# Moving the normalise and residual work of an attention and feed-forward kernel from VectorE to GpSimd, and its last projection one output later

## What is computed

```python
# B = 8, S = 256, D = 128, 16 heads of 8 numbers, hidden size 512
def layernorm(x, eps=1e-5):
    return (x - mean(x)) / sqrt(var(x) + eps)

def attn(x):
    q, k, v = split(x @ W_qkv + b_qkv)
    scores = q @ k.T / sqrt(8) + rel_bias[clip(i - j + 128, 0, 256)]
    return softmax(scores) @ v @ W_out + b_out

def ffn(x):                                  # ternary weights, a scale per output
    h = silu(x @ w1.T * w1_s) * (x @ w2.T * w2_s)
    h = gelu(h @ h1.T * h1_s)
    h = gelu(h @ h2.T * h2_s)
    return h @ w3.T * w3_s

x = x + layernorm(attn(layernorm(x)))
x = x + layernorm(ffn(layernorm(x)))
```

## Time and profile before

| | us |
|---|---|
| median of 3 executions | 291.42 (290.83 to 292.56) |
| the profiled execution | 292.18 |
| its span | 290.4 |
| PE busy | 268.5 (92% of the span) |
| DVE busy | 219.3 (76%) |
| ACT busy | 205.9 (71%) |
| POOL busy | 102.4 (35%) |

### The profile page before, as it was taken

How to read it: one execution, slowest core, us unless ns; L and a number is a source line. 1 busy time by engine, 2 the same in 40 slices (tenths; PEclk the granted TensorE clock), 3 DMA queues, 4 the chain that set the end, 5 groups by cost and what they waited for, 6 DMA issues and landing times.

```text
span 290.4 us, 5171 instructions
## 1 busy us (share of the span) xinstructions
PE 268.5 (92%) x1875; PEld 180.4 (62%) x1875; DVE 219.3 (76%) x442; ACT 205.9 (71%) x316; POOL 102.4 (35%) x107
## 2 busy tenths in 40 slices
PE   7999989899999999999998998899999999999980
PEld 7756645555555554565554554567887888888860
DVE  3489977889789889889889899848556843673674
ACT  2777777776786786885886876777469976896750
POOL 7616000103504305906966957018630202400111
PEclk9999999999999999999999999999999999999996
DMA  6979506232221263470320200000000000010012
GB/s 166 320 238 142 184 11 208 89 83 77 74 76 38 77 207 124 138 224 8 104 81 19 61 1 3 1 3 1 0 2 0 0 0 2 0 36 2 2 36 77
DMA packets 21356, 21.17 MB, mean 73 GB/s; under 512 B 3664, under 2 KB 18768, under 8 KB 21072
## 3 DMA queue, kind: packets, MB, share of 16 engines
q1 hardware_dynamic: 20464, 20.53, 24.8%
q10 hardware_dynamic: 864, 0.27, 0.4%
HBM read 14.90 MB, written 5.64 MB: 71 GB/s over the span
## 4 chain that ended last, share of the span: by engine, by line
PE 60%; DVE 22%; ACT 9%; issue 5%; DMA 1%; POOL 0%; SPq 0%; ACTq 0%; DVEq 0%
PE place L1441 10%; PE place L1442 10%; PE place L1244 8%; DVE mx L685 7%; PE pv L1296 6%; PE place L1236 4%; ACT ring L1008 4%; DVE y_and_z L620 4%; PE place L1270 4%; DVE stats L609 2%; PE place L1195 2%; DVE place L692 2%; ACT place L1015 2%; PE pv L1442 2%; PE pv L1441 2%
## 5 line engine op out<-in xcount | busy, mean ns | idle before, releaser
L685 DVE TENSOR_REDUCE mx<-place 128x4 f32<-128x1024 f32 x64 | 78.1, 1222 | 13.1 <-PE place L1244 11.8
L517 POOL TENSOR_TENSOR rstd<-mv,mhalf 128x2 f32<-128x2 f32 (+1 forms) x26 | 21.0, 809 | 153.0 <-DVE mv L617 153.0
L1008 ACT ACTIVATE ring<-place 128x1024 f32<-128x1024 f32 x64 | 65.6, 1027 | 6.3 <-PE place L1281 3.0
L1244 PE MATMUL place<-room,identr 128*128 128x512 f32 x128 | 46.9, 447 | 0.0
L1015 ACT COPY place<-raw 128x1024 f32<-128x1024 f32 x37 | 37.7, 1022 | 12.2 <-DVE mx L685 11.9
L1441 PE MATMUL place<-room,w_hi 128*128 128x512 f32 (+1 forms) x116 | 44.6, 387 | 0.7 <-DVE room L818 0.7
L1442 PE MATMUL place<-room,w_hi 128*128 128x512 f32 (+1 forms) x116 | 44.0, 382 | 0.0
L818 DVE TENSOR_TENSOR room<-ring,room 128x512 fp32r<-128x512 f32 x32 | 21.4, 690 | 18.5 <-ACT room L1096 18.5
L1296 PE MATMUL pv<-ring,vx 128*9 128x256 f32 x512 | 33.6, 380 | 0.0
L1270 PE MATMUL place<-room 33*128 33x256 f32 x256 | 31.7, 328 | 1.1 <-DVE place L692 1.0
L1236 PE MATMUL place<-room 33*128 33x256 f32 x256 | 28.3, 297 | 2.9 <-ACT ring L1008 2.7
(11 more groups left out here) (141 smaller groups left out, 442.9 us busy)
## 6 DMA issues: line engine op xcount, KB each, us to landing
raw<-ext SPq DMA_DIRECT2D x8, 384.0 KB, 6.9
room<-q_parts SPq DMA_DIRECT2D x48, 64.0 KB
room<-k_parts SPq DMA_DIRECT2D x48, 64.0 KB
w_lo<-h SPq DMA_DIRECT2D x2, 1024.0 KB, 5.2
q_parts<-w_hi SPq DMA_DIRECT2D x4, 256.0 KB, 3.0
k_parts<-w_hi SPq DMA_DIRECT2D x2, 512.0 KB, 3.4
xs<-x SPq DMA_DIRECT2D x3, 256.0 KB, 5.7
w_lo<-w SPq DMA_DIRECT2D x3, 256.0 KB, 2.7
```

Source lines behind the costliest of these rows:

```text
L517: nc.gpsimd.tensor_tensor(rstd[:, at:at + width], mv[:, at:at + width, 1], mhalf[:, 0:width], ALU.pow).then_inc(rstd_set, 1)
L685: nc.vector.tensor_reduce(mx[:, s // RPAIRS, :, :, s % RPAIRS].rearrange("p i k -> p k i"), max_tile(b * PAIRS + s)[:, :, :].rearrange("p ...
L1008: nc.scalar.activation(probs[:, s % PRING, :, :, :].rearrange("p k j n -> p (k j n)"), score_tile(b * PAIRS + s)[:, :, :].rearrange("p k n ...
L1244: last = mm(max_tile(b * PAIRS + s)[:, half, :], identr[:, :], windows(table_hi[:, 2 * s + half, :], 0, P, 2, S), start=False, stop=True, ...
```

## The change

1. POOL takes over the normalising of units 2, 3 and 4 of x, of y and of z, and the addition of the residual. DVE keeps the moments, now as `x1_moments(b - 1)` in slot 6 behind `maxima(b + 1, 6)`; POOL does for each sequence inv_std, two normalise instructions, the addition, inv_std, two normalise instructions, and then the pieces of the weights.
2. DVE normalises unit 0 of x before it takes the moments of unit 1; unit 1 is normalised behind `minus_ident`. POOL does two table copies between the inv_std of unit 1 and of unit 2.
3. PE does the last sequence's projection behind three outputs of layer 1 of chunk 1 in place of two.
4. A wait: before the moments of y of sequence b DVE waits for z of sequence b - 1, since both use the same mean and variance.

The core of the diff (`x_normalize`, `residual` and `second_norm` on DVE are deleted, but for `x_normalize` of units 0 and 1):

```diff
+            def normalize(dst, src, t, at=0):
+                return nc.gpsimd.tensor_scalar(dst, src, mv[:, at + t, 0:1], rstd[:, at + t:at + t + 1],
+                                               ALU.subtract, ALU.mult)
+            def x_normalize(u):
+                first, tiles = UNITS[u]
+                pool.wait_ge(rstd_set, u + 1)
+                if u >= 3:
+                    pool.wait_ge(xnT_ready, 2 if u == 3 else 4)
+                for t in range(tiles):
+                    last = normalize(x_norm[u][:, t, :], xs[:, first + t, :], t, first)
+                last.then_inc(xn_set, 1)
+            def residual(b):
+                inv_std(b * 2 + NU + 1, TPB)
+                pool.wait_ge(rstd_set, b * 2 + NU + 1)
+                for t in range(TPB):
+                    last = normalize(y[:, t, :], y[:, t, :], t)
+                last.then_inc(y_norm, 1)
+                pool.wait_ge(y_norm, b + 1)
+                xb = xs[:, TPB * b:TPB * b + TPB, :]
+                nc.gpsimd.tensor_tensor(xb, xb, y[:, :, :], ALU.add).then_inc(x1_set, 1)
+            def second_norm(b):
+                inv_std(b * 2 + NU + 2, TPB)
+                pool.wait_ge(rstd_set, b * 2 + NU + 2)
+                if b > 0:
+                    pool.wait_ge(zT_ready, b)
+                for t in range(TPB):
+                    last = normalize(z[:, t, :], xs[:, b * TPB + t, :], t)
+                last.then_inc(z_set, 1)
...
             x_inv_std(1)
+            table_high(0)
+            table_high(1)
             x_inv_std(2)
-            for s in range(PAIRS):
+            table_high(2)
+            x_normalize(2)
+            for s in range(3, 6):
                 table_high(s)
-                if s == 5:
-                    x_inv_std(3)
+            x_inv_std(3)
+            x_normalize(3)
+            table_high(6)
+            table_high(7)
...
             x_inv_std(4)
+            x_normalize(4)
...
                 if b > 0:
-                    inv_std((b - 1) * 2 + NU + 1, TPB)
-                    inv_std((b - 1) * 2 + NU + 2, TPB)
+                    residual(b - 1)
+                    second_norm(b - 1)
                 for piece in SPLIT_AT[b]:
                     split_weights(piece)
...
-            inv_std((B - 1) * 2 + NU + 1, TPB)
-            inv_std((B - 1) * 2 + NU + 2, TPB)
+            residual(B - 1)
+            second_norm(B - 1)
             gate_parts(3)
...
-            x_moments(1)
             x_normalize(0)
             dve.wait_ge(row_zeros, 1)
             dve.wait_ge(bq_scaled, 1)
             spread_weights(nc.vector.tensor_copy, 0, (0,))
+            x_moments(1)
...
-            x_normalize(1)
             dve.wait_ge(ident_loaded, 16)
             nc.vector.tensor_scalar(minus_ident[:, :], ident[:, :], -1.0, None, ALU.mult).then_inc(minus_set, 1)
+            x_normalize(1)
...
                 dve.wait_ge(y_read, b + 1)
+                if b > 0:
+
+                    dve.wait_ge(z_set, b)
                 moments(lambda t: y[:, t, :], TPB, b * 6 + base + 2)
...
+            def x1_moments(b):
+
                 dve.wait_ge(x1_set, b + 1)
                 moments(lambda t: xs[:, b * TPB + t, :], TPB, b * 6 + base + 4)
...
-                        if s == 5:
-                            residual(b - 1)
                         if s == 6:
-                            second_norm(b - 1)
+                            x1_moments(b - 1)
...
-                whole(layer1, 1, exact, (0, 1))
+                whole(layer1, 1, exact, (0, 1, 2))
                 project(B - 1)
-                whole(layer1, 1, exact, (2, 3))
+                whole(layer1, 1, exact, (3,))
```

More of the change, by code:

```diff
@@ L630, in x_normalize @@
                 dve.wait_ge(rstd_set, u + 1)
-                if u >= 3:
-                    dve.wait_ge(xnT_ready, 2 if u == 3 else 4)
                 for t in range(tiles):
@@ L716, in attn_moments @@
                 dve.wait_ge(y_read, b + 1)
+                if b > 0:
+                    dve.wait_ge(z_set, b)
                 moments(lambda t: y[:, t, :], TPB, b * 6 + base + 2)
-            def residual(b):
-                dve.wait_ge(rstd_set, b * 2 + NU + 1)
-                for t in range(TPB):
-                    last = normalize(y[:, t, :], y[:, t, :], t)
-                last.then_inc(y_norm, 1)
-                dve.wait_ge(y_norm, b + 1)
-                xb = xs[:, TPB * b:TPB * b + TPB, :]
-                nc.vector.tensor_tensor(xb, xb, y[:, :, :], ALU.add).then_inc(x1_set, 1)
+            def x1_moments(b):
                 dve.wait_ge(x1_set, b + 1)
                 moments(lambda t: xs[:, b * TPB + t, :], TPB, b * 6 + base + 4)
-            def second_norm(b):
-                dve.wait_ge(rstd_set, b * 2 + NU + 2)
-                if b > 0:
-                    dve.wait_ge(zT_ready, b)
-                for t in range(TPB):
-                    last = normalize(z[:, t, :], xs[:, b * TPB + t, :], t)
-                last.then_inc(z_set, 1)
             def z_low(b):
@@ L748, in _ @@
                 if s == 0:
-                    x_normalize(2)
                     keep_v(0)
@@ L754, in _ @@
                     x_moments(3)
-                if s == 3:
-                    x_normalize(3)
                 if s == 6:
@@ L789, in _ @@
                             x_moments(4)
-                        if s == 7:
-                            x_normalize(4)
                     if b > 0:
@@ L863, in _ @@
             layer_low(1, 0, (0, 1))
-            residual(B - 1)
+            x1_moments(B - 1)
             layer_low(1, 0, (2, 3))
-            second_norm(B - 1)
             layer_low(0, 1)
```

## The result

The changed kernel took 306.65 us (median of 4 runs, 302.98 to 313.15), the kernel before, on the same chip, 291.64: a ratio of 1.047 [1.037, 1.057]. That is slower, and 11.65 us above the upper end of the range, 295.0. The profiled execution took 306.09 (span 304.2, against 290.4).

A forecast was written before the change was run, and what follows sets the result against it. PE was taken to bound the kernel, DVE mattering only where PE waits for it. Start +0.4, longer way to z +1.2 and projection -0.7 made +0.9: 292.3 us on the median of 291.42, range 290.0 to 295.0.

The forecast's parts named there:

- The price of a norm: One normalise of 128 columns on POOL was taken as 0.45 us, with 0.3 and 0.75 as ends.
- The rival of dear norms: Loop: a norm on POOL costs 0.5 to 0.75, delaying z in six sequences; likeliest 294.1, at 0.75 295.9; chance 0.35.
- The lower end's estimate: A POOL norm at 0.3: 0.2 fixed plus 0.1 at the cast's rate; the skill's line rate gave a similar sum.
- The longer way to z: Loop: moments follow slot 6's maxima, then POOL's power and norms; sequence 2's transpose at 95.53, not 94.99; +1.2 in all.
- the y side fits: Loop: POOL's power, two y norms and addition take 2.4, done before DVE has finished the maxima of slot 6.
- VectorE's relief: Loop: shedding norms and addition makes slot 6's maxima punctual in sequences 5 and 6, and shortens PE's waits nowhere else.
- Units 2 to 4 of x: Normalising these units on POOL changes nothing, counted at most 0.1, as PE needs them several us later.
- The start: Units 0 and 1: unit 1's norms held up by POOL's table copy, first `row_lows` about 10.9, not 10.51; +0.4.
- The projection: Last sequence's projection one output later: PE does ready matmuls in place of waiting 0.69 for ACT; -0.7.
- The last z: Feed-forward stage: POOL's slower way, 1.3 to 2 more, fits in 3.7 before the transpose unless a norm cost over 1.0.

The follow-up runs named there:

- fill: The changed kernel with 8 dummy matmuls on TensorE ahead of each transpose of z in the loop: 298.31 us, ratio 1.0235.
- fill_more: The changed kernel with 14 dummy matmuls ahead of each wait for z in the loop and 8 at the two last transposes: 299.56 us, ratio 1.0266.
- yz_dve: The changed kernel with the norms of y and z and the addition back on VectorE as before: 290.88 us, ratio 0.9977.
- project_only: The kernel before with only the last sequence's projection moved one output of the feed-forward stage later: 290.74 us, ratio 0.9961.
- late_moments: The kernel before, all norms on VectorE, with only the moments of the sum moved behind the maxima of slot 6: 310.81 us, ratio 1.0623.

## Why the prediction was wrong

**The price of a norm: mis-sized, 0.45 for 0.80.** The upper end, 0.75, was the power of two columns, set aside as another operation; the measured one lies just above it. I took the value nearest to the row with the same operation, by dividing its 1.305 variable part over the columns. But the fixed part came from a cast, and that sum gives 0.53 where 128 columns with two operations and two per-token scalars took 0.80. Whether the fixed part or the second operation and the scalars make the difference, no run tells. The prediction's own rule (each 0.1 on a norm adds 1.2) gives 4.2 more, 296.5, outside its range. The rival of dear norms was the right one, and its price for 0.75, 295.9, was bounded by the same row. The lower end's estimate from the Trainium skill (GPSIMD Engine Reference, Performance versus the Vector engine and Engine selection: one-input work at roughly line rate) is contradicted: by it a norm would be an estimated 0.3, and it took 0.80.

**The longer way to z: the way was right, its lateness too small by the price.** The moments did start behind the maxima (98.06), the power 1.04 behind that, and the wait in sequence 2 was 1.52 where the step makes 0.89 (0.35 + 0.54). The difference, 0.63, is nearly the 0.70 of two norms at 0.35 too little. Measured against before, the transposes of z came 4.7 later by sequence 5, at full clock, in place of the 1.3 of the step; with 0.70 more in each of five sequences the step would have had 4.8. So without the fall of the clock the sum with the right price, 296.5, and the 1.41 of the last z come to 297.9, and `fill` took 298.3. Some of that agreement is chance, for "the y side fits" failed in sequences 5 and 6: power, norms and addition took 3.2 (162.88 to 166.10) where I had 2.4, ended after the maxima, and the waits there grew to 1.93 and 2.33 where I had them under 1.06. And the step took the moments' place as given and never priced it by itself. Set right in the changed kernel it gives back some 8 us, 2 of waiting and 6 of clock; set wrong in the kernel before it costs 19.

**The clock: not in the sum at all, and the largest term.** Before, TensorE's longest wait in the loop was 1.06, and the clock stayed full. I carried waits over as waits, one for one, and no rival had a price that multiplied. `fill` and `fill_more` show that with TensorE busy in the waits the loss falls from some 14 to 15 us to 6.8. The Trainium skill (TensorE: Matmul & The Clock Gate, Why this matters for your kernels) warns of idle gaps between bursts of matmuls, longer ones than any here. The runs agree in kind and differ in size: they show the fall behind waits of 1.4 to 2.4 us. The prediction drew no rival from it.

**VectorE's relief: as forecast, nothing.** It shed 22 us of busy time and TensorE gained none of it. The maxima of slot 6 in sequence 5 were punctual only in the sense that they waited for TensorE.

**Units 2 to 4 of x: nothing, right**: `yz_dve`, which keeps them, is at 290.88 (0.9977 [0.9964, 0.9991]), and the projection alone at 290.74 (0.9961 [0.9947, 0.9974]): no difference that can be told. **The start: +0.1 for +0.4.** Unit 0's second norm ended at 6.48, as reckoned (6.5). Unit 1's norms ended at 9.55, where the step had 9.85, and `row_lows` followed 1.01 behind that, where it had 1.05. **The projection: -0.7, right** in its mechanism; alone it gave 1.1 [0.8, 1.5].

**The last z: failed.** It was said to fit in 3.7 us of cover unless a norm cost over 1.0. The later projection had itself cut the cover, from 3.7 to an estimated 2.8: from the seventh transpose to the last TensorE took 36.34 before (197.06 to 233.40) and 35.41 in `project_only` (197.47 to 232.88). Counted from the seventh transpose, z was done 4.2 later than before. Norms at 0.80 and a power of 0.73 would still have fitted. One norm was held up to 2.23 beside VectorE's subtractions, the other took 1.07 and the power 1.09, 2.1 more in all, and VectorE had idled 2.52 for the addition before. I had priced the norms and the addition (1.3 to 2 more) but not a GpSimd instruction that waits beside VectorE, although show the same the other way round. 1.41 us in place of nothing.

What is left open: why the clock fell behind some waits of 1.5 us and not behind others of 1.9 to 2.3 in the same execution. No run here tells that.

## What to carry to other kernels

Before moving a step to an idler engine, look up what stands next in the queue of the engine it comes back to: a handover that misses a gap in an in-order queue waits for at least a whole instruction of that queue. Here that place alone, with every norm where it was, cost 19 us in the kernel before. Then bound the price of a small instruction by the smallest instructions of that engine, not by scaling a large one. And where TensorE is over 90% busy at full clock, a new wait of 1.5 us is not worth 1.5: in this kernel each microsecond of waiting brought, on average, about another of lost clock.

## What the runs showed of the hardware

- GpSimd's normalisation of 128 columns took 0.79 to 0.80 from any of its three sources when nothing held it up, and an addition of 256 columns 0.73; VectorE took 0.30 to 0.35 for the same norm when GpSimd was quiet.
- The hold-up between the two engines goes both ways: two z norms on VectorE took 1.68 to 1.96 beside GpSimd's weight pieces (0.60 alone), and one norm on GpSimd 2.23 beside VectorE's subtractions.
- In the loop TensorE's clock fell to 1.2 GHz only behind waits of 1.4 to 2.4 us, not behind all of these, and never behind those of up to 1.11. It fell 0.2 to 2.1 us behind the wait (0.2 at 177.6 in `late_moments`) and stayed there for 3 to 14 us (14 from 177.6). With dummy matmuls in the waits the mean clock was that of the kernel before in four executions of five, and with more of them in all four.
- The changed kernel scattered by 10 us (302.98 to 313.15), and with the clock kept full by dummies (`fill_more`) by 0.6 (299.06 to 299.65).
